# A two-layer convolution on one core: ScalarE takes the high parts from the ring, and SyncE's load goes last in its turn

## The reference

```
def _gn(v, G=32, eps=1e-5):          # normalise over 2 channels x 256 x 256
    m, s = mean(g), var(g)
    return (g - m) / sqrt(s + eps)

# layer 0: 3x3 depthwise convolution, then three 64x64 channel mixes
x = x + einsum(G, einsum(pw, einsum(A, depthwise(_gn(x)))))   # A, G: softmaxes of weights
# layer 1: 3x3 convolution of signs with signs, times one mean for each output channel
x = x + conv(sign(_gn(x)), sign(w) * mean(|w|))
```

## Time and profile before

| | us |
|---|---|
| median of 3 runs | 2567.95 |
| lowest, highest | 2565.22, 2568.85 |
| profiled execution | 2559.91 |
| its span, first to last instruction | 2558.0 |

### The profile page before, as it was taken

How to read it: one execution, slowest core, us unless ns; L and a number is a source line. 1 busy time by engine, 2 the same in 40 slices (tenths; PEclk the granted TensorE clock), 3 DMA queues, 4 the chain that set the end, 5 groups by cost and what they waited for, 6 DMA issues and landing times.

```text
span 2558.0 us, 87020 instructions
## 1 busy us (share of the span) xinstructions
PE 2071.0 (81%) x35558; PEld 1486.2 (58%) x35558; DVE 1585.3 (62%) x2510; ACT 1266.7 (50%) x1353; POOL 729.2 (29%) x277
## 2 busy tenths in 40 slices
PE   0499979887798787987879878798687987789976
PEld 0499846555466464665547555565555754567853
DVE  4545557665576655675557656666656666566657
ACT  2244446543465444653446535555345553556544
POOL 0133323332243322432123422234222341234300
PEclk9999989998899998998989999899898998899999
DMA  9632136674466744667346782566725676255436
GB/s 207 147 85 78 47 103 177 177 189 117 117 179 185 196 106 130 178 187 197 79 133 181 190 204 71 141 174 189 199 69 156 176 190 174 68 149 149 125 93 171
DMA packets 310788, 376.14 MB, mean 147 GB/s; under 512 B 22880, under 2 KB 285152, under 8 KB 310496
## 3 DMA queue, kind: packets, MB, share of 16 engines
q1 hardware_dynamic: 310496, 372.01, 56.0%
HBM read 237.71 MB, written 134.22 MB: 145 GB/s over the span
## 4 chain that ended last, share of the span: by engine, by line
PE 32%; DMA 25%; SPq 20%; issue 11%; DVE 7%; ACT 4%; DVEq 1%; ACTq 0%
PE psA L533 28%; DMA out_y<-ring 19%; SPq L219 7%; SPq L228 6%; DMA stats_x<-in_x 5%; SPq L239 4%; PE psB L533 4%; ACT xh L405 2%; SPq L250 2%; DVE ring L839 2%; DVE ring L870 1%; DVE xc L832 1%; DVE suma L864 1%; DVE bnt L701 1%; ACT rnd L426 1%
## 5 line engine op out<-in xcount | busy, mean ns | idle before, releaser
L533 PE MATMUL psA<-xh,W 64*64 64x512 f16 (+1 forms) x19968 | 1566.4, 376 | 331.5 <-ACT xh L405 312.1
L533 PEld LDWEIGHTS psA<-xh,W 64*64 64x64 f16 x19968 | 945.1, 110 | 572.5 <-issue 408.1
L343 POOL TENSOR_TENSOR xl<-xc,xn 128x1024 f16<-128x1024 f32 (+2 forms) x264 | 726.5, 2753 | 1657.1 <-ACT xn L401 1657.1
L533 PE MATMUL psA<-xl,W 64*64 64x512 f16 (+1 forms) x9984 | 1038.9, 368 | 0.2 <-issue 0.2
L533 PEld LDWEIGHTS psA<-xl,W 64*64 64x64 f16 x9984 | 599.9, 109 | 162.5 <-issue 38.6
L401 ACT ACTIVATE xn<-xc 128x1024 f16<-128x1024 f32 (+2 forms) x256 | 270.0, 1055 | 739.4 <-DVE xc L832 734.5
L533 PE MATMUL psB<-pk,W 64*64 64x512 f16 (+3 forms) x5568 | 582.6, 345 | 57.6 <-DVE pk L851 44.8
L839 DVE SCALAR_TENSOR_TENSOR ring<-psA,osc,ring 128x1024 f32<-128x1024 f32 (+1 forms) x256 | 326.7, 1276 | 389.8 <-PE psA L533 389.1
L405 ACT ACTIVATE xh<-xc 64x1024 f16<-64x1024 f32 (+1 forms) x528 | 543.0, 1031 | 9.4
L701 DVE BATCH_NORM_STATS2 bnt<-stats_x 128x6 f32<-128x512 f32 (+1 forms) x392 | 251.6, 684 | 381.9 <-DMA stats_x<-in_x 381.3
L533 PEld LDWEIGHTS psB<-pk,W 64*64 64x64 f16 x5568 | 309.5, 107 | 233.3 <-issue 120.7
(11 more groups left out here) (69 smaller groups left out, 99.2 us busy)
## 6 DMA issues: line engine op xcount, KB each, us to landing
out_y<-ring SPq DMA_DIRECT2D x512, 256.0 KB, 3.5
ring<-in_x SPq DMA_DIRECT2D x452, 256.0 KB, 3.9
stats_x<-in_x SPq DMA_DIRECT2D x392, 256.0 KB, 4.3
ring<-in_x SPq DMA_DIRECT2D x30, 512.0 KB, 14.0
pk<-in_w1T SPq DMA_DIRECT2D x2, 144.0 KB, 7.9
rnd<-in_w1n SPq DMA_DIRECT2D x2, 144.0 KB, 7.7
grp<-in_same_group SPq DMA_DIRECT2D x1, 64.0 KB, 6.2
dwt<-in_dw SPq DMA_DIRECT2D x2, 2.2 KB, 5.8
```

What stands on the lines that cost most here:

```text
L343: ins = nc.gpsimd.tensor_tensor(xl[:, slot:slot + rows, 1:W + 1], xc[:, k:k + rows], xn[:, k:k + rows], ALU.subtract)
L533: mm = pe.matmul(bank[out0:out0 + C, c0:c1], weights[src0:src0 + C, :], src[src0:src0 + C, slot:slot + rows, width[0]:width[0] + width[1]] ...
```

## The change

ScalarE's `high_part` no longer reads xc. It reads the ring and computes rstd0 * x + shift0, with the new value shift0 = -mean0 * rstd0 that VectorE makes once for each image, after which it raises `norm_ready`. It now waits itself for the ring's load, and for xl of the chunk two before. `low_part` waits for xc as well as xn. `normalise` no longer waits for xh, and the step that overwrites mean0 and rstd0 waits for the last xh of the image before. In `turn`, the load of chunk u-2 goes last, behind the store and the statistics' load; for u below 12 it stays in front.

```diff
@@ turn
-                if u.back2 is not None:
+                if u.back2 is not None and u.early:
                     load_chunk(b + 1, u.back2, b * NH + u.back2.half + 1)
+                if u.back1 is not None:
+                    store_chunk(b, u.back1)
                 if stats and u.ahead is not None:
                     load_stats(b + 2, u.ahead)
-                if u.back1 is not None:
-                    store_chunk(b, u.back1)
+                if u.back2 is not None and not u.early:
+                    load_chunk(b + 1, u.back2, b * NH + u.back2.half + 1)
@@ Around
+                    self.early = static and u < 2 * LEAD
@@ low_part
                 pool.wait_ge(xn_rdy, n + 1)
+                pool.wait_ge(xc_rdy, n + 1)
@@ high_part
-                act.wait_ge(xc_rdy, n + 1)
+                if ch.at(0):
+                    act.wait_ge(norm_rdy, img + 1)
+                if not (isinstance(img, int) and img == 0):
+                    landed(img, ch)
+                    if not ch.at(NC - 1):
+                        landed(img, ch.next)
+                if not (isinstance(n, int) and n < 2):
+
+                    act.wait_ge(xl_rdy, n - 1)
...
-                nc.scalar.activation(xn[:, k0:k1], xc[:, k0:k1], ACT.Copy).then_inc(xn_rdy, 1)
+                for at, j, rows in taken(img % 2, ch):
+                    k = buf(ch, j)
+                    ins = nc.scalar.activation(xn[:, k:k + rows], ring[:, ds(at, rows * W)], ACT.Identity,
+                                               bias=shift0[:, 0:1], scale=rstd0[:, 0:1])
+                ins.then_inc(xn_rdy, 1)
                 for (i0, i1), (o0, o1) in ((LO, HI), (HI, LO)):
...
+                                ins = nc.scalar.activation(xh[o0:o1, slot + r0 - j0:slot + r1 - j0, 1:W + 1],
+                                                           ring[i0:i1, ds(at + (r0 - j) * W, (r1 - r0) * W)],
+                                                           ACT.Identity, bias=shift0[i0:i1, 0:1],
+                                                           scale=rstd0[i0:i1, 0:1])
@@ stats_of_group
                     dve.wait_ge(xc_rdy, img * NC)
+                    dve.wait_ge(xh_rdy, img * NC)
...
+                nc.vector.tensor_scalar(shift0[:], mean0[:], rstd0[:, 0:1], -1.0, ALU.mult,
+                                        ALU.mult).then_inc(norm_rdy, 1)
@@ normalise
-                    dve.wait_ge(xh_rdy, n - 1)
                     dve.wait_ge(xl_rdy, n - 1)
```

More of the change, by code:

```diff
@@ L391, in _, with landed @@
             act.wait_ge(pz, 7)
+            def landed(img, ch):
+                act.wait_ge(ld[ch.par], 32 * ((img - 1) * NH + ch.half + 1))
             def high_part(img, ch):
                 n = img * NC + ch.i
-                act.wait_ge(xc_rdy, n + 1)
+                if ch.at(0):
[6 more added lines that the diff above has]
+                    act.wait_ge(xl_rdy, n - 1)
@@ L407, in high_part, with chunk @@
                 ins.then_inc(xh_rdy, 1)
+            def chunk(i, v=0):
+                ch = Chunk(v, i)
+                ch.next = Chunk(v, i + 1)
+                return ch
             def signs(img, ch):
@@ L433, in _ @@
             square_root(0)
-            for i in range(4):
-                high_part(0, Chunk(0, i))
-            with act.Fori(1, NC // 4 - 1) as v:
+            for i in range(8):
+                high_part(0, chunk(i))
+            with act.Fori(2, NC // 4 - 1) as v:
                 for q in range(4):
-                    high_part(0, Chunk(v, q))
+                    high_part(0, chunk(q, v))
             for i in range(NC - 4, NC):
-                high_part(0, Chunk(0, i))
+                high_part(0, chunk(i))
             square_root(1)
-            high_part(1, Chunk(0, 0))
+            high_part(1, chunk(0))
             def steps(b, order):
@@ L449, in steps @@
                     if a1 is not None and a1 > 1:
-                        high_part(b + 1, Chunk(0, a1))
+                        high_part(b + 1, chunk(a1))
                     if u is not None:
@@ L454, in image @@
             def image(b, stats):
-                high_part(b + 1, Chunk(0, 1))
+                high_part(b + 1, chunk(1))
                 signs(b, Chunk(0, 0))
@@ L460, in image @@
                         signs(b, Chunk(v, q + 1))
-                        high_part(b + 1, Chunk(v, q - LEAD + 1))
+                        high_part(b + 1, chunk(q - LEAD + 1, v))
                         round_b(b, Chunk(v, q))
@@ L465, in image @@
                     square_root(b + 2)
-                    high_part(b + 2, Chunk(0, 0))
+                    high_part(b + 2, chunk(0))
             with act.Fori(0, NB - 2) as b:
```

12 lines of the change are left out of this document (6 added, 6 removed).

## The result

| | before | after |
|---|---|---|
| median, us | 2566.59 (4 runs) | 2419.51 (4 runs) |
| lowest, highest | 2558.51, 2568.85 | 2416.87, 2424.67 |
| profiled execution | 2559.91 | 2424.67 |
| its span | 2558.0 | 2422.5 |

The ratio is 0.9435, with a 95% interval of 0.9408 to 0.9461: some 145 us faster, where the prediction had 170. The direction and the range held. The sum behind them did not: it is the difference of terms that were too small and too large, and one had the wrong sign.

The account below looks back on a forecast made before the run. SyncE's queue, waiting each step for a store's landing, was taken to bound the middle at 8.4 us over TensorE's 7.15. Middle 120.6, tail 39 and head 10.5 gave 170 us off, 2398 us; range 2345 to 2480.

Parts of the forecast that it names:

- The closed ring of SyncE: Middle: store landing, load issue and statistics issue make the 8.4 us step; reordering leaves some 5 us, under TensorE's 7.15.
- the statistics tile would fit its two steps: Middle: output chunk to statistics tile to next output takes 11.9 us over two steps, 6.0 a step, under 7.15.
- The collision in the middle: Middle: GpSimd's xl may start ahead of VectorE's output pass and block it; step taken as 7.3 us, bounds 7.15 and 7.73.
- the sign that the prediction gave for being right: Profile after: VectorE's output pass has a mean above 0.85 us, with more instances at 2.67.
- ScalarE from the ring: Head: ScalarE no longer waits for xc, about 1.5 us a turn, 10.5 us in seven turns, bounds 0 and 20.
- I take 0 on the path: ScalarE's activations: pointer operands add latency only, 0 to 0.1 us each, counted as 0.
- The tail: Tail: 6.5 us gained a turn, bounds 2 and 10, six times, 39 us.
- three waits: Tail: transfers start about 3 us earlier, some 2 us of landing wait goes, about 1.5 us from ScalarE not awaiting xc.
- The full collision: Rival, middle: VectorE, once late, stays late and pays the whole block, 7.73 us a step; 2447 us, chance 16%.
- Transfers bind: Rival: DMA at 200 GB/s limits the middle step to 7.87 us and the tail gain to 3; 2484 us, chance 12%.
- Slower: Rival, middle: statistics load queued behind the output chunk, landing at 9 us gives 9.3 a step; 2665 us, chance 4%.
- The sum: Whole kernel: 120.6 us in the middles, 39 in the tails and 10.5 in the heads give 170 us gained.

Follow-up runs that it names:

- SyncE's part alone: The kernel before with only the new order in SyncE's `turn`, ScalarE still reading xc: 2406.87 us, ratio 0.9399.
- ScalarE's part alone: The changed kernel with the old order in SyncE's `turn`: 2567.96 us, ratio 1.0035.
- Half the bytes: The changed kernel loading only the first half of each statistics tile and reading it twice: 2389.96 us, ratio 0.9352.
- moved transfers: The kernel before reordered to statistics, store, load from u = 12, statistics chunks 5 to 9 and ring chunks 0 to 3 loaded in the head: 2319.47 us.
- the one with statistics taken early: The kernel before with order statistics, load, store from u = 12 and statistics of chunks 5 to 9 moved into the head: 2362.77 us, ratio 0.9240.
- the small xl: The changed kernel with GpSimd making xl for one row pair in four, the rest left zero: 2403.06 us, ratio 0.9395.

## Why the prediction was right in sign and range, and where its sum failed

**The closed ring of SyncE.** Right. The landing left the step, and the middle fell to TensorE's floor; SyncE's part alone does all of it (951.3), ScalarE's part alone next to none (1086.3 for 1091.9). That the statistics tile would fit its two steps held as well: 2.7 us of waiting in 19 steps.

**The collision in the middle, predicted 7.3 - 7.15 = 0.15 us a step, 17 us in all.** This term was put too high: a step took 135.89 / 19 = 7.15. The prediction had said that on time nothing moves, and then took part of the price for being late. VectorE was on time. Timeline of one middle step after, beside the earlier trace rows:

```profile
728.34 1.23 ACT L418 ACTIVATE xn<-ring,shift,rstd 128x1024 f16 x1
...
729.38 0.75 DVE L901 SCALAR_TENSOR_TENSOR ring<-suma,wmean,ring 128x512 f32 x1
...
729.65 3.08 POOL L349 TENSOR_TENSOR xl<-xc,xn 128x1024 f16<-128x1024 f32 x1 [4.05 <-ACT xn L418]
```

xl starts 0.27 us behind L901, where it was 0.07 before: the longer xn, the same 0.18 us that cost the heads, keeps the two apart. L901's mean in the second middle is 745 ns, so the sign that the prediction gave for being right, a mean above 0.85 us there, did not come. One of the 19 passes on L898 met xl (their mean is 848 ns). One middle of the seven was over the floor, at 139.5.

**ScalarE from the ring, 10.5 us.** This step was right in sign and size: with pointer operands on both sides the ring gives 10.3 us in seven heads, without them 15.4. That the first agrees to 0.2 us is luck. Waits for xh fell by 4.7 and 6.2 us, TensorE's busy time by 14.7 and 8.5, at a higher clock, and with pointers other waits took a part back. The prediction had no term for the clock.

**"I take 0 on the path" for the pointer operands.** This is the step that failed, and the largest miss. It rested on the earlier trace rows: sg has one pointer operand, takes 1.14 us beside 1.04, and the next one starts 1.04 later, so the difference was read as latency. That row shows an activation followed by one of another kind. sg overlaps xn by the same 0.10 us in the changed kernel (727.30, 1.14 long, and xn at 728.34), so its interval was 1.04 with a pointer, and the row has none without one to set beside it. What counted was the interval from one with two pointers to the next, 1.26 us for 1.08, three times a chunk, 0.53 us where ScalarE is what TensorE waits for. In the second head TensorE waits 18.4 us for xh in the changed kernel, 16.8 with SyncE's part alone, four times in each. Seven heads pay 26 to 31 us, somewhat over half of it in these waits and the rest in TensorE's busy time at a lower clock, of a term that had 0 and bounds of 0.1 us each. The prediction looked at the clock in the middles alone. In the middle ScalarE has 35 us to spare (100.17 busy of 135.89), and the same 0.53 us a step costs nothing.

**The tail, 39 us, measured 16.6.** The prediction had the bounds 2 and 10 a turn and took 6.5; it was 2.8 in each of six (57.8 to 55.0). SyncE's part alone gave 2.3, where 5 were counted, and ScalarE's part alone nothing (386.1 for 386.2), where 1.5 were. The rate was the reason it gave for the lower bound, and it binds. DMA of the changed kernel from 826.2 to 862, in 40 slices, then the queue's packets, MB and share:

```profile
GB/s 140 212 228 167 293 227 238 227 191 211 213 182 302 179 252 260 253 229 208 235 246 249 233 220 261 225 221 222 224 238 245 251 228 229 252 235 217 235 238 224
DMA packets 5733, 8.18 MB, mean 228 GB/s; under 512 B 489, under 2 KB 4833, under 8 KB 5729
...
q1 hardware_dynamic: 5729, 8.12, 100.0%
```

The share is 1.00 over 36 us, so starting some 3 us earlier and dropping a wait could only move the queue, not the bytes: 8.12 MB at 228 GB/s. The prediction counted 13 transfers and 6.8 MB, 30 us at 222 GB/s, and still took 6.5 off. The step that failed is the taking of three waits as gain beside a resource that was already full behind them. Half the bytes (55.0 to 49.6) and moved transfers (to 40.2) confirm that the transfers hold the tail. The order counts as well, by what it leaves behind the tail's last store: eleven half-megabyte transfers for statistics, load, store (50.9 us), twelve for statistics, store, load (52.4), thirteen for the change's order (55.5 in SyncE's part alone). One is 0.52 MB, 2.3 us at 228 GB/s, and two of them are the 4.6 us between first and last, though the steps are 1.5 and 3.1. This count is argued and not shown: the kernel before leaves eleven as well, with tails of 57.8, and the one with statistics taken early leaves six, with 47.9. The change's order is the worst of the three there, which the prediction did not count.

**The rivals.** The full collision did not come. "Transfers bind" was true in the tail and false in the middle, where 215 GB/s at a share of 0.90 was enough; half the statistics' bytes left the middle alone. "Slower" stood on a tile's landing over 7.1 us. These are the landings in the second middle (KB, median us from issue):

```profile
out_y<-ring SPq DMA_DIRECT2D x38, 256.0 KB, 3.3
stats_x<-in_x SPq DMA_DIRECT2D x36, 256.0 KB, 4.3
ring<-in_x SPq DMA_DIRECT2D x36, 256.0 KB, 4.8
```

They are far from it. What was missing was a rival in which ScalarE's longer activations make the head slower.

**The sum.** 170 + 16.4 (middle) - 27.6 (heads) - 22.4 (tails) - 1.2 (image 0) = 135. That the total missed by no more than this is in part luck, since the middle's miss ran against the other two.

## What to carry to other kernels

Look in an in-order DMA queue for a wait for a landing with issues of other kinds behind it: if landing and issues add up to the step, putting the independent transfer in front of that wait takes the step to the next bound, 8.4 to 7.15 us here. Where transfers fill a stretch, earlier starts give little; move transfers to a stretch in which the queue idles, and those first that stand behind a wait for a landing. An operand that replaces a dependency is paid on each instruction, so price it by the start-to-start interval of the very form, on the stretch where that engine is waited for, and look at TensorE's granted clock in that stretch too. Here the small edit of an activation ate twice what the removed dependency gave.

## What the runs showed of the hardware

- **An activation of 1024 columns** starts the next 1.26 us later as Identity with two pointer operands and 1.08 as Copy without (xn to xh).
- **Longer waits of TensorE came with a lower clock.** With pointer operands seven heads waited 16 and 17 us longer for xh, and TensorE was busy 17 and 11 us longer with the same products, with 41 and 24 us more at the lower clock level.
- **Which of VectorE's passes stands behind GpSimd.** No row of before showed it for the first output pass, which reads int16 and float32 from SBUF. The changed kernel's tail does:

```profile
828.75 2.69 DVE L898 SCALAR_TENSOR_TENSOR ring<-rnd,wmean,ring 128x512 f32<-128x512 int16 x1
...
828.76 2.14 POOL L349 TENSOR_TENSOR xl<-xc,xn 128x1024 f16<-128x1024 f32 x1 [5.00 <-ACT xn L418]
```

  It takes 2.69 us for 0.75, with the two starts 0.01 us apart, and ends 0.5 us behind xl. In reverse, with the VectorE pass first (729.38, above), GpSimd's takes 3.08 us for 2.14. The Trainium skill, SBUF — State Buffer, section Who interferes with whom, says that a VectorE instruction with two SBUF inputs competes with GpSimd's. The traces agree: the sums with one input from PSUM (L870) kept their 1.28 us, four of them beside a running xl. One more instruction stood, with a single SBUF input: `normalise` once a turn (2.62 us for 0.81 at 680.59, where xl had started at 679.70); with the small xl it took 1.16.
- **Loads of 256 KB landed within 4.3 and 4.8 us** (statistics, ring) at 215 GB/s and a share of 0.90, against 4.2 and 3.9 at 183 GB/s and 0.68, and within 5.0 and 6.0 in the tail at 228 GB/s and 1.00 (medians).
